# Cross-attention layers on one core: the second head group's fetch at unit 37, the context's load in parts

## Chip, cores and metric

The kernel runs on one core of one Trainium2 chip. The metric is device time in microseconds of one execution, as the median of several.

## What is computed

Two cross-attention layers over the same context, for 8 batches of 256 text rows by 256 features and a context of 1601 rows by 256 features. Cut to what matters, everything in float32:

```python
def layer0(x, ctx):                       # 16 heads of 16 features
    a = layernorm(ctx) * gamma + beta
    Q, K, V = x @ Wq.T, a @ Wk.T, a @ Wv.T
    return x + tanh(gate) * (softmax(Q K.T / 4) V) @ Wo.T

def layer1(x, ctx):
    q = layernorm(x) @ q_w + q_b
    k, v = ctx @ k_w + k_b, ctx @ v_w + v_b
    h = x + (softmax(q k.T / 4) v) @ cproj_w + cproj_b
    return h + gelu(layernorm(h) @ fc_w + fc_b) @ proj_w + proj_b
```

The mask of the first layer is all ones in the data.

## The kernel before

**Blocks and units.** One block is the attention of one layer for one batch; there are 16, numbered n = 0 to 15, even ones for layer 0, odd ones for layer 1. In the program a block is known by `n0`: 0 and 1 stand alone, 2 and 3 are the body of a loop of six passes, 14 and 15 stand alone again; -1 and 16 are a prologue and an epilogue without attention. An odd block here is n0=1 or n0=3. n0=14 is an even block by its attention, but it prepares the keys of the last odd block.

A block has 52 units: four groups of four heads (g = 0 to 3), times 13 tiles of 128 context rows. In a unit TensorE makes the scores of the tile for four heads in two halves, ScalarE takes the exponentials, and TensorE weighs the values with them one unit later. Beside that a unit holds one or two chunks: the scores of 128 queries against all 1601 keys, of which VectorE takes the maximum for the softmax. The chunks run 22 ahead, so at unit 47 those of the next block's second group begin. Two chunk buffers stand between TensorE and VectorE: a chunk waits until the maximum two chunks earlier has been taken.

**Pieces.** While block n attends, it also prepares the next one and finishes the previous one, in pieces put at fixed units by tables (`PREP0_AT`, `PREP1_AT`, `POST0_AT`, `POST1_AT`): T (transpose two tiles of the context), K(m, c) (keys of head half m, context chunk c), Q, V, WO, FC and PJ (the MLP), MX (transpose the maxima of a group; units 9, 22, 35, 48). In a block that prepares layer 1 Q is at unit 23, K(1,0) to K(1,3) at 25, 28, 30 and 33, FC at 12, 17, 27 and 32, V(0) at 36.

**A K piece's way.** TensorE multiplies; ScalarE saves a rounded first part into one of two buffers `parts`; VectorE makes the remainder and a second part, GpSimd the third (bf16 parts that add up to the float32 value); SyncE stores the three to HBM (`split_out`, 384 KB). A piece uses the buffer of the piece before the last, so ScalarE's save waits until that store has landed.

**SyncE's queue.** SyncE issues nearly all DMAs, in program order, each after its waits: `split_out`; `maxima_move` (a store, a wait for it, a load); `fetch_keys` and `fetch_queries`, which read a head group's parts back into the operands `kst` and `qst` (7 and 6 DMAs); `ctx_load`, which reads a batch's context into `ctxn`; x and the output. `FETCH_AT` gives the units at which the first, second and third group of the next block are fetched; the fourth is fetched as the next block starts. `CTX_LOAD_AT` gives the unit of the context's load in even and in odd blocks.

**Who reads the context.** The context that an odd block loads is first read in the same block by VectorE: its statistics (`ctx_stat_tiles`), two tiles at each of the units of `STATS_AT`, the first pair at unit 31, after that unit's maximum and ahead of the next ones:

```python
STATS_AT = {31: 0, 32: 1, 34: 2, 36: 3, 38: 4, 40: 5, 44: 6}
```

The context that an even block loads (the same batch's, unnormalized) is first read by TensorE, in piece T(0) at unit 1 of the next block.

Of the kernel before, what the change touches and what calls it, by code (L numbers as in the profile page):

```python
# [29 lines left out]
B, T, S, D, H, DH, FF = 8, 256, 1601, 256, 16, 16, 1024  # L30
NT = -(-S // P)
LAST = S - (NT - 1) * P
FULL = (NT - 1) * P
# [48 lines left out]
STATS_AT = {31: 0, 32: 1, 34: 2, 36: 3, 38: 4, 40: 5, 44: 6}  # L82

CTX_LOAD_AT = (43, 23)

FIRST = ([("XT",)] + [("T", k) for k in range(7)] + [("K", 0, c) for c in range(4)]
         + [("Q",), ("V", 0), ("V", 1), ("V", 2), ("V", 3), ("V", 4), ("K", 1, 0), ("K", 1, 1), ("MX", NG), ("V", 5),
# [2 lines left out]
FIRST_CHUNKS = {("MX", NG): range(16), ("V", 5): range(16, 18), ("K", 1, 2): range(18, 20),  # L90
                ("K", 1, 3): range(20, 21), ("V", 6): range(21, 16 + EARLY)}

FETCH_AT = (24, 26, 40)


class Block:
# [96 lines left out]
def chunk_cols(c):  # L193
    return 4 * P if c < 3 else LAST
# [27 lines left out]
def build(nc, x, ctx, mask, Wq0, Wk0, Wv0, Wo0, gamma0, beta0, gate, ln1_w, ln1_b, q_w, q_b, k_w, k_b, v_w, v_b,  # L222
# [11 lines left out]
    with es:  # L234
        def sb(name, shape, dt=F32):
            return es.enter_context(nc.sbuf_tensor(name, shape, dt))

        def sem(name):
            return es.enter_context(nc.semaphore(name))
# [22 lines left out]
        ctxn = sb("ctxn", [P, NT, D])  # L262
# [61 lines left out]
        scores_ready = sem("scores_ready")  # L324
# [12 lines left out]
        misc_ready = sem("misc_ready")  # L337
# [7 lines left out]
        ctx_in = sem("ctx_in")  # L345
# [30 lines left out]
        def hold(engine, signal, value):  # L376


            engine.wait_ge(signal, value)

        def attended_batch(blk):
            return {0: 0, 1: 1, 2: blk.i, 3: blk.i + 2, 14: 6, 15: 7}[blk.n0]

        def next_ctx(blk):

            if blk.n0 == 3:
                j = blk.i + 3
                return j - j // B
            return {-1: 1, 0: 0, 1: 2, 2: blk.i + 1}[blk.n0]
# [2 lines left out]

            return blk.i + (2 if blk.n0 == 1 else 3)

        def ctx_load(sp, blk_b, after_misc):

            if after_misc is not None:
                hold(sp, misc_ready, after_misc)
            sp.dma_start(ctxn[:, 0:NT - 1, :], ctx[blk_b, 0:FULL, :].rearrange("(p j) d -> p j d", j=NT - 1)
                         ).then_inc(ctx_in, 16)  # L400
            sp.dma_start(ctxn[0:LAST, NT - 1, :], ctx[blk_b, FULL:S, :]).then_inc(ctx_in, 16)

        @block.sync
        def _(sp):
            for dst, w in (*zip(raw_qkv, (Wq0, Wk0, Wv0)), (raw_wo, Wo0)):
                sp.dma_start(dst, w.rearrange("(c o) i -> o c i", o=P)).then_inc(raw_loaded, 16)
            sp.wait_ge(const_made, 1)
            ctx_load(sp, 0, None)
            with nc.allow_non_contiguous_dma(reason="feature vectors as columns, once"):
                for dst, src in ((c_g0, gamma0), (c_b0, beta0)):  # L410
                    sp.dma_start(dst, src.rearrange("(c p) -> p c", p=P)).then_inc(raw_loaded, 16)
# [36 lines left out]
            def place_bias_rows():  # L448

                sp.wait_ge(row_saved, 2)  # L450
                for l in range(2):
                    sp.dma_start(wo[l][DH:DH + 1, 0, :], bias_row[:, l, :]).then_inc(rows_placed, 16)
# [23 lines left out]
            def fetch_keys(n, blk, k, blk_b, first):  # L476

                hs = slice(HG * k, HG * k + HG)
                for buf in range(2):
                    hold(sp, parts_out[buf], 16 * blk.uses_through(3 if k < 2 else 8, buf))  # L480
                if not first:
                    hold(sp, scores_ready, 104 * (n - 1) + 26 * (k + 1))
                m = k // 2
                rows = slice(DH * hs.start - P * m, DH * hs.stop - P * m)
                for j, (_, kp) in enumerate(PARTS):
                    sp.dma_start(kst[product_rows(j), hs, :], scr_k[m, kp, rows].rearrange("(h d) s -> d h s", d=DH)  # L486
                                 ).then_inc(k_in[k], 16)
                sp.dma_start(kst[RP:RP + 1, hs, :], scr_mask[blk_b].unsqueeze(0).unsqueeze(0).broadcast_to([1, HG, S])
                             ).then_inc(k_in[k], 16)

            def fetch_queries(blk, k):

                hs = slice(HG * k, HG * k + HG)
                for buf in range(2):
                    hold(sp, parts_out[buf], 16 * blk.uses_through(4 if k < 2 else 8, buf))
                m = k // 2
                rows = slice(DH * hs.start - P * m, DH * hs.stop - P * m)
                for j, (qp, _) in enumerate(PARTS):
                    sp.dma_start(qst[product_rows(j), hs, :], scr_q[qp, m, rows].rearrange("(h d) t -> d h t", d=DH)  # L499
                                 ).then_inc(q_in[k], 16)  # L500
# [13 lines left out]
            def visit(blk):  # L514
                n = blk.n
                if blk.n0 == 0:
                    place_bias_rows()
                if 0 <= blk.n0 < 16:

                    maker = Block(blk.n0 - 1, blk.i, None, 0, None, 0)  # L520
                    fetch_keys(n, maker, 3, attended_batch(blk), blk.n0 == 0)
                    fetch_queries(maker, 3)
                if blk.n0 == 0:
                    sp.dma_start(xin[1][:, :, :], x[1].rearrange("(p t) d -> p t d", t=TT)).then_inc(x_in, 16)
                units = range(UNITS) if blk.attends else [u for u in blk.at]
                for u in units:
                    piece = blk.at.get(u)
                    kind = piece[0] if piece else None
                    if kind in ("K", "Q"):
                        split_out(blk, piece)  # L530
                    if piece == ("WO", 1) and blk.post == 0 and blk.prep == 0:
                        hold(sp, misc_saved, blk.misc(piece) + 1)
                        sp.dma_start(xin[1][:, :, :], x[blk.prep_b].rearrange("(p t) d -> p t d", t=TT)
                                     ).then_inc(x_in, 16)
                    if kind == "MX":
                        if blk.post == 1 and piece[1] == NG:

                            hold(sp, y_out, 16 * (blk.post_b + 1))
                        maxima_move(blk, piece[1])
                    if blk.n0 < 14 and (u == CTX_LOAD_AT[blk.par] if blk.attends else piece == ("K", 1, 1)):  # L540
                        ctx_load(sp, next_ctx(blk), blk.misc(("T", NT // 2)) + 1)
                    if piece == ("PJ", 1):
                        hold(sp, misc_saved, blk.misc(piece) + 1)
                        sp.dma_start(out[blk.post_b].rearrange("(p t) d -> p t d", t=TT), y[:, :, :]
                                     ).then_inc(y_out, 16)
                    if blk.prep is not None and blk.attends and u in FETCH_AT:
                        fetch_keys(n + 1, blk, FETCH_AT.index(u), blk.prep_b, False)
                        fetch_queries(blk, FETCH_AT.index(u))
                    if blk.n0 < 0 and piece == ("K", 0, 3):
                        fetch_keys(n + 1, blk, 0, blk.prep_b, True)  # L550
                    if blk.n0 < 0 and piece == ("Q",):
                        fetch_queries(blk, 0)
                        fetch_keys(n + 1, blk, 1, blk.prep_b, True)
                        fetch_queries(blk, 1)
                    if blk.n0 < 0 and piece == ("K", 1, 3):
                        fetch_keys(n + 1, blk, 2, blk.prep_b, True)
                        fetch_queries(blk, 2)

            walk(visit)
            sp.wait_ge(y_out, 16 * B)  # L560

# [257 lines left out]
        def _(dve):  # L819
# [79 lines left out]
            def ctx_stat_tiles(blk, js, ahead):  # L899

                if js[0] == 0:
                    dve.wait_ge(ctx_in, 32 * (blk.n + 1 + ahead))
                    if blk.n0 < 0:
                        dve.wait_ge(const_made, 1)
                for j in js:
                    ins = dve.bn_stats(st[:, j, :], ctxn[:, j, :])
                if js[-1] == NT - 1:
                    ins.then_inc(ctx_stats, 1)
# [81 lines left out]
            def visit(blk):  # L990
                if not blk.attends and blk.prep == 0:
                    ctx_stat_tiles(blk, range(NT), 1)
                    ctx_var_all(blk.prep_b)
                    fold_first()
                    ctx_apply(dve, blk, range(NT))
# [57 lines left out]
        def _(pe):  # L1053
# [98 lines left out]
            def do_piece(blk, piece):  # L1152
# [4 lines left out]
                if kind == "T":  # L1157
                    k = piece[1]
                    js = range(2 * k, min(2 * k + 2, NT))
                    if blk.prep == 0:  # L1160
                        pe.wait_ge(ctx_normed, NT * blk.prep_b + js[-1] + 1)
                    elif k == 0:
                        pe.wait_ge(ctx_in, 32 * (blk.n + 2))
                    for j in js:
                        r = tile_rows(j)
                        for c in range(CH):
# [3 lines left out]
                elif kind == "K":  # L1170
                    mo, ck = piece[1:]
                    w = chunk_cols(ck)
# [4 lines left out]
                elif kind == "V":  # L1177
                    k = piece[1]
# [110 lines left out]
```

## Time and profile before

| | us |
|---|---|
| median of three runs | 2037.35 |
| the three runs | 2036.52, 2037.35, 2040.63 |
| the profiled execution | 2044.37 |
| its span | 2042.5 |
| TensorE busy | 1960.1 (96%) |
| VectorE busy | 1417.5 (69%) |
| ScalarE busy | 1298.0 (64%) |
| GpSimd busy | 424.1 (21%) |

The span is what the profile shows of the execution, from its first to its last instruction. An engine is busy while it executes; register, branch, semaphore and DMA-issuing instructions are not counted. Matmuls overlap and their ends are modelled, so a busy TensorE is not TensorE at its peak. Engines are called PE (TensorE), PEld (its weight loads), DVE (VectorE), ACT (ScalarE), POOL (GpSimd) and SP or SPq (SyncE and its DMA issues) in rows.

### The profile page before, as it was taken

Reading aid. Unit: us, or ns where it says so; the run is one execution under the profiler, and the core shown is the slowest. Engines: PE = TensorE matmul, PEld = TensorE weight load, DVE = VectorE, ACT = ScalarE, POOL = GpSimd, SP = SyncE. Lnnn points to the kernel's source line nnn. Section 1 sums busy time; section 2 is a strip of 40 time slices with the busy share of each in tenths; the row PEclk is TensorE's granted clock in tenths of the full one; section 3 lists DMA queues with packets and bytes.
Section 4 is the critical chain, followed back from the end, with each engine's and each line's share of the span. In section 5 each row is a group of like instructions: output and inputs, shape, how many; then the busy total and the mean of one; then the engine's idle time right before and its main releaser. Section 6 shows DMA issues by size and latency. Waiting matters only on the chain.

```text
span 2042.5 us, 38305 instructions
## 1 busy us (share of the span) xinstructions
PE 1960.1 (96%) x14940; PEld 1053.3 (52%) x14940; DVE 1417.5 (69%) x2389; ACT 1298.0 (64%) x2327; POOL 424.1 (21%) x441
## 2 busy tenths in 40 slices
PE   5899999999999999999999999999999999999996
PEld 4345545455554545555554555545555554554544
DVE  3677777767677776777767676686767777676742
ACT  2166656667666675667756676666766667665773
POOL 2041113103141132311232022310323103111110
PEclk8799989999999999999999999999999999999998
DMA  6435152341515242251522515143241525214100
GB/s 150 126 83 150 45 140 54 97 107 58 123 43 129 68 126 60 54 150 37 138 63 71 130 35 149 41 112 92 79 102 51 129 60 139 63 37 114 30 7 6
DMA packets 142698, 176.01 MB, mean 86 GB/s; under 512 B 35092, under 2 KB 113085, under 8 KB 140469
## 3 DMA queue, kind: packets, MB, share of 16 engines
q1 hardware_dynamic: 140373, 170.67, 32.0%
q10 hardware_dynamic: 2144, 2.90, 0.6%
q8 instruction: 118, 1.93, 0.4%
q14 instruction: 63, 0.52, 0.1%
HBM read 125.33 MB, written 48.16 MB: 85 GB/s over the span
## 4 chain that ended last, share of the span: by engine, by line
PE 76%; DVE 6%; SPq 5%; ACT 5%; DMA 4%; POOL 3%; issue 2%; ACTq 0%
PE p_sc L1114 18%; PE p_acc L1147 18%; PE p_mx L1134 14%; PE p_misc L1182 9%; PE p_misc L1175 6%; DMA scr_k<-parts 3%; PE p_misc L1220 2%; PE p_misc L1208 2%; PE p_misc L1168 2%; DVE maxes L869 2%; SPq L499 2%; SPq L486 2%; PE p_misc L1214 2%; ACT prob L779 2%; DVE rest L949 2%
## 5 line engine op out<-in xcount | busy, mean ns | idle before, releaser
L869 DVE TENSOR_REDUCE maxes<-p_mx 128x1 f32<-128x802 f32 x1024 | 985.7, 984 | 336.1 <-PE p_mx L1134 332.1
L779 ACT ACTIVATE prob<-p_sc 128x512 f32<-128x512 f32 (+1 forms) x1664 | 963.1, 596 | 328.7 <-PE p_sc L1114 326.7
L1114 PE MATMUL p_sc<-qst,kst 100*128 100x256 bf16 (+1 forms) x3328 | 647.3, 276 | 23.3 <-ACT prob L779 22.1
L1134 PE MATMUL p_mx<-kst,qst 97*128 97x401 bf16 x2048 | 528.0, 339 | 10.1 <-DVE maxes L869 9.2
L1147 PE MATMUL p_acc<-prob,vals 128*17 128x256 f32 x6656 | 523.1, 386 | 0.2
L1114 PEld LDWEIGHTS p_sc<-qst,kst 100*128 100x128 bf16 (+1 forms) x3328 | 262.0, 99 | 505.5 <-ACT prob L779 215.1
L622 POOL TENSOR_TENSOR parts<-rest,parts 128x512 bf16<-128x512 f32 (+1 forms) x144 | 139.7, 970 | 638.5 <-DVE parts L960 638.4
L1147 PEld LDWEIGHTS p_acc<-prob,vals 128*17 128x17 f32 x6656 | 110.4, 95 | 243.4 <-issue 195.2
L1134 PEld LDWEIGHTS p_mx<-kst,qst 97*128 97x128 bf16 x2048 | 192.9, 99 | 54.3 <-DVE maxes L869 26.3
L1182 PE MATMUL p_misc<-wv,ctxt 128*128 128x256 f32 x800 | 193.5, 383 | 2.0 <-DVE rest L949 2.0
L1175 PE MATMUL p_misc<-ctxt,wk 128*128 128x512 f32 x488 | 191.1, 514 | 1.4 <-ACT vals L733 0.7
L643 POOL TENSOR_TENSOR o_t<-o_raw,o_den 128x256 f32<-128x256 f32 x64 | 46.6, 729 | 628.0 <-DVE o_den L897 628.0
L1182 PEld LDWEIGHTS p_misc<-wv,ctxt 128*128 128x128 f32 x800 | 144.3, 188 | 23.9 <-DVE rest L949 2.4
L949 DVE SCALAR_TENSOR_TENSOR rest<-p_misc,cols,parts 128x512 f32<-128x512 f32 x122 | 76.7, 629 | 109.7 <-ACT parts L715 108.2
L733 ACT ACTIVATE vals<-p_misc 128x512 f32<-128x512 f32 (+1 forms) x108 | 61.1, 566 | 139.9 <-PE p_misc L1182 139.9
L715 ACT ACTIVATE parts<-p_misc,cols 128x512 bf16<-128x512 f32 x122 | 72.3, 593 | 110.7 <-PE p_misc L1175 89.3
L897 DVE RECIPROCAL o_den<-o_den 128x128 f32<-128x128 f32 x128 | 120.4, 942 | 0.1
L591 POOL TENSOR_SCALAR ctxn<-ctxn,mv,rstd 128x256 f32<-128x256 f32 x91 | 110.0, 1222 | 0.8
L1175 PEld LDWEIGHTS p_misc<-ctxt,wk 128*128 128x128 f32 x488 | 81.7, 191 | 53.7 <-issue 44.8
L1208 PE MATMUL p_misc<-wo,o_t 128*128 128x256 f32 x248 | 60.5, 387 | 3.6 <-issue 3.6
L1168 PE MATMUL p_misc<-ident,ctxn 128*128 128x128 f32 (+1 forms) x398 | 60.8, 272 | 3.0 <-POOL ctxn L591 1.2
L1214 PE MATMUL p_misc<-x_t,wfc 128*128 128x256 f32 x240 | 59.2, 391 | 1.4 <-ACT x_t L738 0.7
(143 smaller groups left out, 1084.3 us busy)
## 6 DMA issues: line engine op xcount, KB each, us to landing
kst<-scr_k SPq DMA_DIRECT2D x384, 200.1 KB
scr_k<-parts SPq DMA_DIRECT2D x96, 384.0 KB, 3.1
ctxn<-in_ctx_dram SPq DMA_DIRECT2D x16, 1536.0 KB
qst<-scr_q SPq DMA_DIRECT2D x384, 32.0 KB, 2.9
scr_q<-parts SPq DMA_DIRECT2D x16, 384.0 KB, 3.1
xin<-in_x_dram SPq DMA_DIRECT2D x8, 256.0 KB, 2.8
out_dram<-y SPq DMA_DIRECT2D x8, 256.0 KB, 2.0
scr_k<-parts SPq DMA_DIRECT2D x32, 48.8 KB, 2.3
```

The costliest lines, as they stand in the source:

```text
L591: engine.tensor_scalar(ctxn[:, j, :], ctxn[:, j, :], mv[:, j, 0:1], rstd[:, j:j + 1], ALU.subtract, ALU.mult).then_inc(ctx_normed, 1)
L622: pool.tensor_tensor(parts[buf][:, 2, 0:w], rest[:, buf, 0:w], parts[buf][:, 1, 0:w], ALU.subtract).then_inc(low_ready, 1)
L779: act.activation(prob[0:rows, u % 2, 2 * half:2 * half + 2, :].rearrange("p h t -> p (h t)"), p_sc[0:rows, half, :], ACT.Exp).then_inc(exp ...
L869: dve.tensor_reduce(maxes[:, c:c + 1], p_mx[:, c % 2, :, 0:CW], AX.XY, ALU.max).then_inc(chunk_done, 1)
L897: dve.reciprocal(o_den[:, half], o_den[:, half]).then_inc(den_step, 1)
L949: dve.scalar_tensor_tensor(out=rest[:, buf, 0:w], in0=res[:, 0:w], scalar=bias, in1=parts[buf][:, 0, 0:w], op0=ALU.add, op1=ALU.subtract). ...
L1114: ins = mm(p_sc[0:rows, half, T * q:T * q + T], kst[0:RB, h, P * j:P * j + rows], qst[0:RB, h, :], start=True, stop=True)
L1134: ins = mm(p_mx[:, c % 2, w, 0:CW], qst[0:RA, h, P * t:P * t + P], kst[0:RA, h, s0:s0 + CW], start=True, stop=True)
L1147: ins = mm(p_acc[32 * q:32 * q + VW, 0:T], vals[par][0:rows, j, h, :], prob[0:rows, u % 2, q, :], start=(j == 0), stop=(j == NT - 1))
L1168: ins = nc.tensor.transpose(res[:, o:o + r], ctxn[0:r, j, P * c:P * c + P], ident[0:r, 0:r])
L1175: ins = mm(res[:, 0:w], wk[blk.prep][:, c, P * mo:P * mo + P], rhs, start=(c == 0), stop=(c == CH - 1))
L1182: ins = mm(res[0:r, o:o + D], ctxt[:, j, c, 0:r], wv[blk.prep][:, c, :], start=(c == 0), stop=(c == CH - 1))
```

## The change

The second group's fetch is made at unit 37 instead of 26 and the third's at 41 instead of 40. The context's load, before one transfer of 12 tiles and one of the last 65 rows, becomes four transfers of three tiles and that of the last rows; in a block with attention they stand two units apart, at units 23, 25, 27, 29 and 31 of an odd block and 43 to 51 of an even one, each behind a wait for the scores of the unit before. The first load (at the start) and the second (in the prologue) are made in the same five transfers, one behind the other. The readers wait for all five.

```diff
--- before.py
+++ after.py
@@ -82,6 +82,8 @@
 STATS_AT = {31: 0, 32: 1, 34: 2, 36: 3, 38: 4, 40: 5, 44: 6}
 
 CTX_LOAD_AT = (43, 23)
+CTX_PARTS = 4
+CTX_STEP = 2
 
 FIRST = ([("XT",)] + [("T", k) for k in range(7)] + [("K", 0, c) for c in range(4)]
          + [("Q",), ("V", 0), ("V", 1), ("V", 2), ("V", 3), ("V", 4), ("K", 1, 0), ("K", 1, 1), ("MX", NG), ("V", 5),
@@ -90,7 +92,7 @@
 FIRST_CHUNKS = {("MX", NG): range(16), ("V", 5): range(16, 18), ("K", 1, 2): range(18, 20),
                 ("K", 1, 3): range(20, 21), ("V", 6): range(21, 16 + EARLY)}
 
-FETCH_AT = (24, 26, 40)
+FETCH_AT = (24, 37, 41)
 
 
 class Block:
@@ -392,20 +394,23 @@
 
             return blk.i + (2 if blk.n0 == 1 else 3)
 
-        def ctx_load(sp, blk_b, after_misc):
-            if after_misc is not None:
-                hold(sp, misc_ready, after_misc)
-            sp.dma_start(ctxn[:, 0:NT - 1, :], ctx[blk_b, 0:FULL, :].rearrange("(p j) d -> p j d", j=NT - 1)
+        def ctx_load(sp, blk_b, k):
+            if k == CTX_PARTS:
+                sp.dma_start(ctxn[0:LAST, NT - 1, :], ctx[blk_b, FULL:S, :]).then_inc(ctx_in, 16)
+                return
+            w = (NT - 1) // CTX_PARTS
+            js = slice(w * k, w * k + w)
+            sp.dma_start(ctxn[:, js, :], ctx[blk_b, 0:FULL, :].rearrange("(p j) d -> p j d", j=NT - 1)[:, js, :]
                          ).then_inc(ctx_in, 16)
-            sp.dma_start(ctxn[0:LAST, NT - 1, :], ctx[blk_b, FULL:S, :]).then_inc(ctx_in, 16)
 
         @block.sync
         def _(sp):
             for dst, w in (*zip(raw_qkv, (Wq0, Wk0, Wv0)), (raw_wo, Wo0)):
                 sp.dma_start(dst, w.rearrange("(c o) i -> o c i", o=P)).then_inc(raw_loaded, 16)
             sp.wait_ge(const_made, 1)
-            ctx_load(sp, 0, None)
+            for k in range(CTX_PARTS + 1):
+                ctx_load(sp, 0, k)
             with nc.allow_non_contiguous_dma(reason="feature vectors as columns, once"):
                 for dst, src in ((c_g0, gamma0), (c_b0, beta0)):
                     sp.dma_start(dst, src.rearrange("(c p) -> p c", p=P)).then_inc(raw_loaded, 16)
@@ -537,8 +542,13 @@
 
                             hold(sp, y_out, 16 * (blk.post_b + 1))
                         maxima_move(blk, piece[1])
-                    if blk.n0 < 14 and (u == CTX_LOAD_AT[blk.par] if blk.attends else piece == ("K", 1, 1)):
-                        ctx_load(sp, next_ctx(blk), blk.misc(("T", NT // 2)) + 1)
+                    for k in range(CTX_PARTS + 1):
+                        if blk.n0 < 14 and (u == CTX_LOAD_AT[blk.par] + CTX_STEP * k if blk.attends else piece == ("K", 1, 1)):
+                            if k == 0:
+                                sp.wait_ge(misc_ready, blk.misc(("T", NT // 2)) + 1)
+                            if blk.attends:
+                                sp.wait_ge(scores_ready, 104 * n + 2 * u)
+                            ctx_load(sp, next_ctx(blk), k)
                     if piece == ("PJ", 1):
                         hold(sp, misc_saved, blk.misc(piece) + 1)
                         sp.dma_start(out[blk.post_b].rearrange("(p t) d -> p t d", t=TT), y[:, :, :]
@@ -899,7 +909,7 @@
             def ctx_stat_tiles(blk, js, ahead):
 
                 if js[0] == 0:
-                    dve.wait_ge(ctx_in, 32 * (blk.n + 1 + ahead))
+                    dve.wait_ge(ctx_in, 16 * (CTX_PARTS + 1) * (blk.n + 1 + ahead))
                     if blk.n0 < 0:
                         dve.wait_ge(const_made, 1)
                 for j in js:
@@ -1160,7 +1170,7 @@
                     if blk.prep == 0:
                         pe.wait_ge(ctx_normed, NT * blk.prep_b + js[-1] + 1)
                     elif k == 0:
-                        pe.wait_ge(ctx_in, 32 * (blk.n + 2))
+                        pe.wait_ge(ctx_in, 16 * (CTX_PARTS + 1) * (blk.n + 2))
                     for j in js:
                         r = tile_rows(j)
                         for c in range(CH):
```

In the rows below, which show the order of instructions, the names are those of the tensors: `scr_k` and `scr_q` hold the stored parts of keys and queries, `kst` and `qst` the operands, `scr_max` the maxima, `ctxn` the context. First SyncE in the first odd block (n0=1), from Q's store on (the loop's odd blocks read alike). Before:

```order
L464 DMA scr_q<-parts 128x6x256
L399 DMA ctxn<-in_ctx_dram 128x3072
L401 DMA ctxn<-in_ctx_dram 65x256
L486 DMA kst<-scr_k 16x4x1601 x6
L488 DMA kst<-scr_mask 1x4x1601
L499 DMA qst<-scr_q 16x4x256 x6
L473 DMA scr_k<-parts 128x3x512
L486 DMA kst<-scr_k 16x4x1601 x6
L488 DMA kst<-scr_mask 1x4x1601
L499 DMA qst<-scr_q 16x4x256 x6
L473 DMA scr_k<-parts 128x3x512 x2
L473 DMA scr_k<-parts 128x3x65
```

And now:

```order
L469 DMA scr_q<-parts 128x6x256
L404 DMA ctxn<-in_ctx_dram 128x768
L491 DMA kst<-scr_k 16x4x1601 x6
L493 DMA kst<-scr_mask 1x4x1601
L504 DMA qst<-scr_q 16x4x256 x6
L478 DMA scr_k<-parts 128x3x512
L404 DMA ctxn<-in_ctx_dram 128x768 x2
L478 DMA scr_k<-parts 128x3x512
L404 DMA ctxn<-in_ctx_dram 128x768
L478 DMA scr_k<-parts 128x3x512
L400 DMA ctxn<-in_ctx_dram 65x256
L478 DMA scr_k<-parts 128x3x65
```

The second group's 13 DMAs (`kst`, `scr_mask`, `qst`) have left the place between the first and second of the four stores `scr_k<-parts`, and the parts of the context (`128x768`, at the end `65x256`) stand between the stores instead; the last part comes behind the third store.

Then SyncE in the even block n0=0, from the store of K(1,3) on. Before:

```order
L473 DMA scr_k<-parts 128x3x65
L486 DMA kst<-scr_k 16x4x1601 x6
L488 DMA kst<-scr_mask 1x4x1601
L499 DMA qst<-scr_q 16x4x256 x6
L399 DMA ctxn<-in_ctx_dram 128x3072
L401 DMA ctxn<-in_ctx_dram 65x256
L508 DMA scr_max<-max_rows 24x128
L511 DMA qst<-scr_max 3x1024
```

And now:

```order
L478 DMA scr_k<-parts 128x3x65
L491 DMA kst<-scr_k 16x4x1601 x6
L493 DMA kst<-scr_mask 1x4x1601
L504 DMA qst<-scr_q 16x4x256 x6
L491 DMA kst<-scr_k 16x4x1601 x6
L493 DMA kst<-scr_mask 1x4x1601
L504 DMA qst<-scr_q 16x4x256 x6
L404 DMA ctxn<-in_ctx_dram 128x768 x3
L513 DMA scr_max<-max_rows 24x128
L516 DMA qst<-scr_max 3x1024
L404 DMA ctxn<-in_ctx_dram 128x768
L400 DMA ctxn<-in_ctx_dram 65x256
```

The second group's fetch, which stood further up, is now between that store and the third group's, and the context's fourth and fifth parts come behind the move of the maxima of unit 48.

Last VectorE, in the first odd block of the changed kernel, from K(1,2) at unit 30 on, with what each row waits for:

```order
L959 SCALAR_TENSOR_TENSOR rest<-p_misc,cols,parts 128x512 [waits low_ready,high_ready]
L970 CAST parts<-rest 128x512 [waits misc_saved]
L879 TENSOR_REDUCE maxes<-p_mx 128x1 [waits chunk_ready]
L916 BN_STATS st<-ctxn 128x6 [waits ctx_in]
L916 BN_STATS st<-ctxn 128x6
L879 TENSOR_REDUCE maxes<-p_mx 128x1 [waits chunk_ready]
L916 BN_STATS st<-ctxn 128x6 x2
L879 TENSOR_REDUCE maxes<-p_mx 128x1 [waits chunk_ready]
L886 TENSOR_REDUCE neg_max<-maxes 128x8 [waits chunk_done]
```

These rows and their order are those of before; what has moved is the last of the transfers that the first BN_STATS, at unit 31, waits for.

## Rows read from the trace of the kernel before

**Rows 1.** The page, part 1, whole span: busy time, share, instructions by engine.

```profile
PE 1960.1 (96%) x14940; PEld 1053.3 (52%) x14940; DVE 1417.5 (69%) x2389; ACT 1298.0 (64%) x2327; POOL 424.1 (21%) x441
```

**Rows 2.** Waits over the whole span: engine, line, awaited, us in total, times, longest.

```profile
ACT parts L715 <- DMA scr_k<-parts: 33.5, 14, 11.3
```

**Rows 3.** Timeline of TensorE, six stretches: start, us, instruction, idle before and releaser.

```profile
285.92 0.39 PE L1114 MATMUL p_sc<-qst,kst 100*128 100x256 bf16 x2 [2.89 <-ACT prob L779]
...
522.41 0.39 PE L1114 MATMUL p_sc<-qst,kst 100*128 100x256 bf16 x2 [0.66 <-ACT prob L779]
...
1005.69 0.39 PE L1114 MATMUL p_sc<-qst,kst 100*128 100x256 bf16 x2 [1.07 <-ACT prob L779]
1012.77 0.39 PE L1114 MATMUL p_sc<-qst,kst 100*128 100x256 bf16 x2 [0.28 <-ACT prob L779]
...
1017.10 0.63 PE L1147 MATMUL p_acc<-prob,vals 128*17 128x256 f32 x8
...
1730.69 0.39 PE L1114 MATMUL p_sc<-qst,kst 100*128 100x256 bf16 x2 [1.01 <-ACT prob L779]
...
1860.77 0.49 PE L1114 MATMUL p_sc<-qst,kst 100*128 100x256 bf16 x2 [4.16 <-ACT prob L779]
...
1868.23 0.63 PE L1147 MATMUL p_acc<-prob,vals 128*17 128x256 f32 x8
```

**Rows 4.** Timeline of ScalarE at the saves of key projections, three blocks.

```profile
284.69 0.69 ACT L715 ACTIVATE parts<-p_misc,cols 128x512 bf16<-128x512 f32 x1 [5.30 <-DMA scr_k<-parts]
...
1004.46 0.69 ACT L715 ACTIVATE parts<-p_misc,cols 128x512 bf16<-128x512 f32 x1 [1.16 <-DMA scr_k<-parts]
...
1859.91 0.32 ACT L715 ACTIVATE parts<-p_misc,cols 128x65 bf16<-128x65 f32 x1 [5.07 <-DMA scr_k<-parts]
```

**Rows 5.** Timeline of SyncE's DMA issues, an odd block and block n0=14.

```profile
988.13 0.54 SPq L399 DMA_DIRECT2D ctxn<-in_ctx_dram  x1
...
997.99 0.52 SPq L473 DMA_DIRECT2D scr_k<-parts  x1
...
1008.23 5.34 SPq L473 DMA_DIRECT2D scr_k<-parts  x3
...
1855.94 5.62 SPq L473 DMA_DIRECT2D scr_k<-parts  x3
```

**Rows 6.** Timeline of VectorE, then GpSimd, in the same odd block.

```profile
1005.97 0.43 DVE L960 CAST parts<-rest 128x512 bf16<-128x512 f32 x1
...
1007.21 0.74 DVE L906 BATCH_NORM_STATS2 st<-ctxn 128x6 f32<-128x256 f32 x2
...
1011.49 0.17 DVE L885 TENSOR_TENSOR max_parts<-neg_max,max_parts 128x8 bf16<-128x8 f32 x1
...
1012.27 0.29 DVE L949 SCALAR_TENSOR_TENSOR rest<-p_misc,cols,parts 128x65 f32<-128x65 f32 x1 [0.62 <-ACT parts L715]
...
1006.47 1.16 POOL L622 TENSOR_TENSOR parts<-rest,parts 128x512 bf16<-128x512 f32 x1 [4.58 <-DVE parts L960]
```

**Rows 7.** Timeline of TensorE, the transposition of the maxima at unit 35.

```profile
1013.10 0.23 PE L1224 MATMUL p_misc<-ident_h,max_parts 128*24 128x128 bf16 x1
```

**Rows 8.** SyncE's waits; the chain at 48.93 (start, us); SyncE's timeline after it.

```profile
SPq L511 <- DMA scr_max<-max_rows: 88.0, 64, 3.4
...
48.93 3.04 DMA scr_k<-parts
...
48.93 0.89 SPq L473 DMA_DIRECT2D scr_k<-parts  x2
52.60 0.62 SPq L486 DMA_DIRECT2D kst<-scr_k  x1
```

**Rows 9.** Windows: us, busy time by engine, TensorE's granted clock, DMA share, GB/s.

```profile
288.00:290.00 2.00, 2.00 (x12) 1.43 (x14) 2.00 (x5) 1.20 (x2) 0.00 (x0) 0.50 0.60 159
1972.00:1976.00 4.00, 3.04 (x28) 1.09 (x28) 0.21 (x1) 3.59 (x7) 1.27 (x1) 1.00 0.03 7
```

**Rows 10.** Timeline of TensorE, its first instruction.

```profile
13.77 1.94 PE L1062 MATMUL p_sc<-ident,ctxt 128*128 128x128 f32 x8 [13.77 <-DMA cols<-in_L_xattn_ln_beta_dram]
```

## The prediction

> **What bounds the kernel now.** I read the page first: TensorE is busy for 1960.1 of 2042.5 us [rows 1]. That is a queue worked off in order, with few holes, so a gain can only come from the holes, and a loss only from new ones. The list of waits then tells what this change can reach: ScalarE stands 33.5 us, in 14 waits, before it saves a key projection, for a store of an earlier projection to land (its buffer is still being read) [rows 2]. TensorE's own timeline shows which of these reach it [rows 3]. In each of the six odd blocks of the loop it has one hole of 0.66 to 1.07 us behind the stalled ScalarE, in the block shown a second one of 0.28; in the first odd block (n0=1) a hole of 2.89; in the block n0=14 one of 4.16. The rest of the 33.5 us lies in the prologue and in block 0.
>
> The cause is seen on SyncE, one queue in order [rows 5]. In an odd block it issues Q's store, the context's load (1.5 MB) at 988.13, 13 DMAs of the first head group, then the store of piece K(1,0) at 997.99, 13 DMAs of the second group, and only at 1008.23 the stores of K(1,1), K(1,2) and K(1,3). ScalarE's save of K(1,2) needs K(1,0)'s store landed: it starts at 1004.46, 6.5 us after that store was issued, having waited 1.16 [rows 4]. In n0=14 there is no context load, and the fetch alone does it: K(1,1)'s store is issued at 1855.94 [rows 5], and ScalarE's save of K(1,3) waits 5.07 for it [rows 4].
>
> After the two long holes TensorE runs at half its clock: a granted share of 0.50 in 288 to 290 us, which is the level of 1.2 GHz, against 1.00 (2.4 GHz) elsewhere in the loop, as in 1972 to 1976 [rows 9]. In n0=14 the work from 1860.77 to 1868.23 takes 7.46 us; the same work (from unit 35's scores to the weighing after V(0)) takes 4.33 in a block at full clock, 1012.77 to 1017.10 [rows 3]. So that hole costs 4.16 + 3.1 = **7.3 us**.
>
> **The fetch at unit 37 instead of 26, the third at 41.** The 26 DMAs are the same. The stores of K(1,1) to K(1,3) no longer stand behind 13 issues (1008.23 less 998.5: nearly 10 us). In n0=14 K(1,1)'s store is issued right behind K(1,0)'s, some 8 us earlier, lands after about 3 us (a store of this size took 3.04 [rows 8]) and is there before ScalarE, which stood ready at 1859.91 - 5.07 = 1854.84 [rows 4]. The hole goes whole: **-7.3 us** (-4.2 if another wait keeps the clock low). The second group's keys are first read at unit 47 of the same block, ten units later; 13 issues take about 8.5 us (9.86 for 15, 988.13 to 997.99 [rows 5]) and two units took 4.33 [rows 3], so some 20 us cover them. The third group's are read in the next block, at its unit 8. In odd blocks that fetch now also stands behind the wait for the output of the MLP at unit 41; with 19 units to go it costs nothing, and TensorE would stand for it only if SyncE were held some 20 us longer.
>
> **The context's load in parts.** K(1,0)'s store now has 0.4 MB of context ahead of it, not 1.6. By the 3.04 us it lands near 1001, before ScalarE needs it (1004.46 - 1.16 = 1003.30) [rows 4, 8]. So the 1.16 us, and the 1.07 and 0.28 us of TensorE behind it [rows 3], go away in every odd block.
>
> But the load now ends later than its reader. VectorE starts the statistics of the new context at unit 31 and waits there for all five transfers. The fifth is issued at unit 31 on SyncE, behind the store of K(1,2), and that store waits for VectorE and GpSimd to split K(1,2). Step by step in the block at 1004, with everything 1.16 us earlier:
> - VectorE's cast of K(1,2) ended at 1005.97 + 0.43, now at 1005.24; GpSimd's subtraction ended at 1006.47 + 1.16, now at 1006.47 [rows 6].
> - SyncE then issues the store and, some 0.6 us later (0.54 for an issue [rows 5]), the fifth part: 1007.1.
> - It lands after x. No row shows a 65 KB load behind a store. From below: a 6 KB store on an empty queue is waited for 88.0/64 = 1.4 us [rows 8]. From above: in the prologue two stores are issued from 48.93, the first large, the second small; the first lands after 3.04, and the next instruction that waits for both starts at 52.60, so the small one took at most 3.2 us from its own issue near 49.4 [rows 8]. That is the nearest case (a small transfer 0.5 us behind a large store); I take **x = 2.7**: landing at 1009.8.
> - VectorE has done its maximum of unit 31 by 1006.2 and stands 3.6 us. Queued behind are all maxima of later units, two of which TensorE may be ahead of, then the split of the maxima and K(1,3)'s first step, which TensorE's transposition of the maxima at unit 35 waits for.
> - From the first statistic to the last step of that split VectorE needed 1007.21 to 1011.66, then 0.29 for K(1,3) [rows 6]; without the short waits inside, with the releases, 4.65 us. TensorE's transposition so comes at 1014.45, where it came at 1013.10 [rows 7]: **+1.35 us a block**, in general x - 1.35.
>
> Bounds for the block: x = 1.4 gives 0, x = 3.2 gives 1.85; if VectorE's delay were wholly hidden, -1.35. TensorE makes the delay up nowhere, since it has no other holes. Six blocks: **+8.1 us** (0 to +11).
>
> The Trainium skill (DMA: Bandwidth & Descriptors, Queues, rings and completion order) says that a transfer's completion count lands only after every earlier write of the same DMA engine. By that the fifth part could not count before K(1,2)'s store is done, and the sum would stay at or above what x = 2.5 gives, +6.9 us for the six blocks. The bound of 3.2 us agrees with it; no row here shows a load counted behind a store.
>
> **The block n0=1.** ScalarE has less to do there and waited 5.30 [rows 4]. The store of K(1,0) now lands some 2.4 us sooner, so the statistics wait until about 288.7 and the transposition comes half a microsecond sooner than before. TensorE still has a hole, now of some 3 to 4 us in place of 2.89, so it still drops to half clock, and a V piece comes to lie in the slow stretch: about +1.3. Together **+0.8** (-3 to +3).
>
> **The rest.** At the start three more issues (0.5 each) stand ahead of the norm's vectors, for which TensorE waits until 13.77 [rows 10]. They lie in the same queue behind the weights and the whole context in either kernel, so I take the data and not the issue to set their time: +0.1, at most +1.6 were the cover gone. In even blocks the parts go out at units 43 to 51 and TensorE transposes the first tile at unit 1 of the next block, two units or some 4.3 us after the last is issued; against 2.7 us for landing that is hidden; uncovered, the price would be what landing takes beyond that, once in each pair of blocks. Two further issues a load in SyncE's idle time: nothing.
>
> **Sum**: -7.3 + 8.1 + 0.8 + 0.1 = **+1.7 us**. The profiled execution took 2044.37 us with 2042.5 of span; the three timed runs have a median of 2037.35, which is 0.34% less. I put the difference on the median: **2039 us**. Own range of this case 2033 to 2046.
>
> **Rivals.**
> A. *The forecast*: the wait moves from ScalarE to VectorE, the gain of n0=14 is given back in the six blocks. 45%.
> B. *Faster*: the fifth part lands soon, or VectorE's delay is taken up by TensorE's two units of slack. Then the six blocks give 6 x -1.35 = -8, n0=14 -7.3, n0=1 its 2.89 and the some 4 us of slow clock behind it: -22, or 2015. It decides at x of about 1.4; at x = 2 the sum is -7.3 + 3.9 + 0.8 = -2.5. For it: the 6 KB row. Against: the two stores of the prologue. 18%.
> C. *Slower, by the clock*: in the six blocks TensorE would have, by the steps above, about 1.5 us idle at unit 34, 1.4 us of work, 1.4 us idle at unit 35. If that takes it to half clock as in n0=14, each such block loses another 3.1 us: all six +18.6, the sum +20, 2058; three of them 2048. For it: the holes of 2.89 and 4.16 us did it. Against: holes of 1.07 and less did not, nor a stretch with 3.04 of 4 us busy, 1972 to 1976, at 1.00 [rows 9]. This lies between, so some blocks may drop and others not. 30%. The Trainium skill (TensorE: Matmul & The Clock Gate, HAM oscillation — how this bites in real kernels) describes a kernel whose waits take it to the lower clock anew in every tile. By that rule the time would be this case's, near 2058.
> D. *The gain of n0=14 does not come*, since another wait takes the place of K(1,3)'s: +9, 2046. 7%.
>
> **Chances.** A change under 0.2% (4 us) is what a measurement of this kernel can't tell. A lies mostly inside it (36 of 45, with 6 slower, 3 faster); B is faster (16 of 18); C slower (26 of 30); D slower (5 of 7). Faster 0.19, within 0.44, slower 0.37 (the remainders of B, C and D are put within). The range leaves out the whole of B's far end and the last of C: **2024 to 2057**.
>
> **What would show it.** Right: in the odd blocks VectorE's statistics at unit 31 wait 3 to 4 us for the context's DMA, ScalarE's waits for the stores of keys are gone, TensorE's holes lie at units 34 and 35 and are VectorE's; n0=14 has no hole and no slow stretch. Wrong: no such wait of VectorE (B); a granted clock under 1.00 in the odd blocks of the loop (C); a save still waiting for a store in n0=14 (D); or a hole at the first transposition of an odd block, which I put at nothing.

## The result: 2047.64 us, 0.4% more, and a time that follows the clock

| | before | changed |
|---|---|---|
| median, timed on the same chip | 2037.64 us (2036.41 to 2042.43, 6 runs) | 2047.64 us (2037.75 to 2052.92, 6 runs) |
| ratio | | 1.004, 95% interval 1.0025 to 1.0055 |
| the profiled execution, its span | 2044.37, 2042.5 us | 2037.75, 2035.9 us |
| mean granted clock of that execution | 0.981 | 0.984 |

The profiled execution of the changed kernel happens to be the quickest of its six, and it is quicker than the profiled one of before. So the profile shows what the change does while the clock holds, and the medians show that something else is added in most executions. Both have to be explained.

The profile after, first its list of waits over the whole span (engine, line, awaited, us in total, times, longest):

```profile
DVE st L916 <- DMA ctxn<-in_ctx_dram: 24.4, 7, 3.6
...
PE p_mx L1144 <- DVE maxes L879: 18.2, 31, 3.1
...
ACT parts L725 <- DMA scr_k<-parts: 13.8, 4, 9.3
...
PE p_misc L1234 <- DVE rest L959: 6.9, 6, 1.1
```

ScalarE's wait for stores of keys fell from 33.5 us in 14 waits [rows 2] to 13.8 in 4, of which one (3.13 us, in n0=1) is not in the prologue or block 0. A new wait stands on top: VectorE, seven times, once in each odd block that loads a context. Next SyncE's timeline in the first odd block of the loop, with the issues that were [rows 5]:

```profile
510.72 0.52 SPq L478 DMA_DIRECT2D scr_k<-parts  x1
511.29 1.11 SPq L404 DMA_DIRECT2D ctxn<-in_ctx_dram  x2
514.09 0.38 SPq L478 DMA_DIRECT2D scr_k<-parts  x1
514.51 0.49 SPq L404 DMA_DIRECT2D ctxn<-in_ctx_dram  x1
519.78 0.38 SPq L478 DMA_DIRECT2D scr_k<-parts  x1
520.20 0.46 SPq L400 DMA_DIRECT2D ctxn<-in_ctx_dram  x1
```

The stores are no longer behind 13 issues, but the fourth part of the context is issued at 514.51 and the fifth only at 520.20, right behind K(1,2)'s store. VectorE's timeline in the same place (start, us, instruction, idle before and releaser):

```profile
518.44 0.98 DVE L879 TENSOR_REDUCE maxes<-p_mx 128x1 f32<-128x802 f32 x1
522.84 0.75 DVE L916 BATCH_NORM_STATS2 st<-ctxn 128x6 f32<-128x256 f32 x2 [3.42 <-DMA ctxn<-in_ctx_dram]
...
526.97 0.28 DVE L959 SCALAR_TENSOR_TENSOR rest<-p_misc,cols,parts 128x65 f32<-128x65 f32 x1
```

It has nothing to do from 519.42 to 522.84, which is 2.64 us after the fifth part's issue. TensorE's timeline, in n0=1, in that block, and in n0=14:

```profile
287.28 0.85 PE L1144 MATMUL p_mx<-kst,qst 97*128 97x401 bf16 x2 [3.08 <-DVE maxes L879]
...
524.54 0.52 PE L1144 MATMUL p_mx<-kst,qst 97*128 97x401 bf16 x2 [1.03 <-DVE maxes L879]
...
527.30 0.23 PE L1234 MATMUL p_misc<-ident_h,max_parts 128*24 128x128 bf16 x1 [1.15 <-DVE rest L959]
...
1857.94 0.39 PE L1124 MATMUL p_sc<-qst,kst 100*128 100x256 bf16 x2
...
1862.26 0.63 PE L1157 MATMUL p_acc<-prob,vals 128*17 128x256 f32 x8
```

Each of the six odd blocks of the loop has this pair of holes, the first 0.95 to 1.18 us, the second 1.14 or 1.15, in place of the two short ones of before (0.66 to 1.07 us, then 0.28 to 0.64). In n0=14 the hole of 4.16 us is gone, and the work from unit 35's scores to the weighing after V(0) takes 4.32 us instead of 7.46. Last the granted clock in windows of 2 us (us, busy by engine, clock, DMA share, GB/s):

```profile
288.00:290.00 2.00, 2.00 (x13) 0.36 (x11) 1.82 (x7) 0.60 (x1) 0.00 (x0) 0.50 0.00 0
...
528.00:530.00 2.00, 2.00 (x19) 1.21 (x18) 2.00 (x6) 1.43 (x3) 1.10 (x1) 1.00 0.19 27
530.00:532.00 2.00, 2.00 (x17) 1.13 (x16) 1.61 (x4) 2.00 (x4) 1.28 (x1) 1.00 0.04 9
```

In this execution TensorE drops to 1.2 GHz (0.50) behind n0=1's hole, but behind none of the six pairs.

### The profile page after: what moved, and what is told of

The parts are those of the page before. It is cut to its first block, busy times and chain, and to the rows that moved or that the text cites. A ratio compares the mean times of both kernels' runs of the same rounds, so it can differ in the third digit from the quotient of the medians.

```text
span 2035.9 us, 38367 instructions
## 1 busy us (share of the span) xinstructions
PE 1954.9 (96%) x14940; PEld 1049.2 (52%) x14940; DVE 1416.0 (70%) x2389; ACT 1297.6 (64%) x2327; POOL 423.2 (21%) x441
## 4 chain that ended last, share of the span: by engine, by line
PE 80%; DVE 8%; ACT 5%; POOL 3%; DMA 2%; issue 2%; SPq 1%; ACTq 0%
PE p_acc L1157 19%; PE p_sc L1124 19%; PE p_mx L1144 15%; PE p_misc L1192 9%; PE p_misc L1185 7%; DVE maxes L879 3%; PE p_misc L1230 2%; PE p_misc L1218 2%; PE p_misc L1224 2%; PE p_misc L1178 2%; DVE rest L959 2%; ACT parts L725 2%; ACT prob L789 1%; PE p_misc L1211 1%; POOL parts L632 1%
```

## The experiments

Two theories were to be told apart. **Theory 1** is the forecast's mechanism: VectorE waits for the context's last part, TensorE for VectorE, and what the pair of holes costs depends on whether the clock then falls. **Theory 2**: the transfers themselves (more of them, or the second group's later fetch) cost the time, and the wait is hidden. Ratios are to the kernel before on the same chip, with the 95% interval; its median was 2039.59 us beside experiments 1 to 4 (16 runs) and 2040.46 beside 5 to 8 (11 runs).

**1. The changed kernel again, unedited.**

> The changed kernel unaltered, to see what its scatter (2037.75 to 2052.92 us in six executions) goes with. Theory 1 (the clock): the two holes of TensorE that VectorE's wait for the context makes in each odd block take it to half clock in some blocks and not in others, so the time follows the mean granted clock: about 2038 us at 0.984 and 2050 at 0.976 to 0.978, with half-clock stretches behind the holes in the profile where the time is high. Theory 2 (the transfers): the later fetch and the parts of the context collide differently from run to run; the time then differs at the same granted clock, and the waits for DMA differ between the two profiles by 5 us or more.

2056.13 us (2039.19 to 2059.54, 11 runs), ratio 1.0066 (1.0044 to 1.0088). The runs line up with their mean granted clock: 2039.19 us at 0.983, 2044.57 at 0.981, 2051.10 at 0.980, 2056.13 at 0.974, 2059.54 at 0.972 (in the order of the clocks some runs between 2056 and 2059 change places). The one that was profiled took 2056.13 us. TensorE's timeline in its first and last odd block of the loop, then windows behind the pairs:

```profile
528.89 0.52 PE L1144 MATMUL p_mx<-kst,qst 97*128 97x401 bf16 x2 [1.33 <-DVE maxes L879]
531.66 0.28 PE L1234 MATMUL p_misc<-ident_h,max_parts 128*24 128x128 bf16 x1 [1.15 <-DVE rest L959]
...
1754.85 0.52 PE L1144 MATMUL p_mx<-kst,qst 97*128 97x401 bf16 x2 [1.08 <-DVE maxes L879]
1757.62 0.23 PE L1234 MATMUL p_misc<-ident_h,max_parts 128*24 128x128 bf16 x1 [1.15 <-DVE rest L959]
```

```profile
532.00:534.00 2.00, 2.00 (x12) 0.46 (x11) 2.00 (x5) 0.81 (x2) 1.45 (x2) 0.50 0.18 25
534.00:536.00 2.00, 2.00 (x11) 1.29 (x8) 1.01 (x2) 1.69 (x4) 0.86 (x1) 0.50 0.04 6
...
1758.00:1760.00 2.00, 2.00 (x19) 1.10 (x18) 2.00 (x5) 1.15 (x2) 1.41 (x2) 1.00 0.21 32
```

It is the same program with nearly the same holes, but now the clock is at 0.50 behind four of the six pairs for some 6.8 us each (530 to 538 is the first), behind a fifth for half as long (1512 to 1518), and behind the last not at all. From the first pair to the last this execution needed 1754.85 - 528.89 = 1225.96 us, the earlier one 1736.75 - 524.54 = 1212.21: 13.75 more for four and a half drops, or **3.06 us a drop**. The other 4.6 us between the two executions lie mostly at the start: an early hole of 0.82 us stands at 114.26 here and at 110.57 there. The waits for DMA differ by less than the 5 us that theory 2 asked for: VectorE's for the context add up to 25.2 us here and 24.4 there, ScalarE's for stores of keys to 16.3 and 13.8.

**2. Only the fetch moved** (the context's load as before):

```diff
-FETCH_AT = (24, 26, 40)
+FETCH_AT = (24, 37, 41)
```

> Only the fetches moved, the context's load as before. Theory 1: the gain of block n0=14 comes whole (-7.3 us), the 0.7 to 1.1 us holes of the odd blocks stay, since the store of K(1,0) still stands behind the whole context; no wait of VectorE for the context. 2030 us, with little scatter. Theory 2: the fetch at unit 37 brings the scatter, so runs from 2030 to 2045.

2027.34 us (2025.39 to 2036.08, 6 runs), ratio 0.9952 (0.9935 to 0.997). This half of the change is a gain. The runs are less steady than theory 1 expected: four lie from 2025.39 to 2027.59 at a clock of 0.985 to 0.987, two at 2034.10 and 2036.08 with 0.982 and 0.979. No profile shows one of those two. In the profiled execution (2025.39) the hole of n0=14 is gone. In n0=1 ScalarE still waits 4.62 us for the store, and TensorE has two holes, six us apart, without a fall of the clock between them (timeline of TensorE, then a window):

```profile
282.81 0.39 PE L1114 MATMUL p_sc<-qst,kst 100*128 100x256 bf16 x2 [2.22 <-ACT prob L779]
...
288.79 0.23 PE L1224 MATMUL p_misc<-ident_h,max_parts 128*24 128x128 bf16 x1 [0.85 <-DVE rest L949]
```

```profile
284.00:286.00 2.00, 2.00 (x26) 1.09 (x18) 2.00 (x5) 1.72 (x4) 0.75 (x1) 1.00 0.16 54
```

The context's load in one piece still delays the stores in the loop: ScalarE waits 0.27 to 1.35 us in five of the six blocks. So the second group's later fetch by itself doesn't cost time, and the loss of the whole comes in with the load in parts.

**3. Only the load in parts** (the changed kernel with the fetch put back):

```diff
-FETCH_AT = (24, 37, 41)
+FETCH_AT = (24, 26, 40)
```

> Only the context's load in five parts, the fetches as before. Theory 1: the fifth part now stands behind the second group's fetch too, so VectorE waits longer at unit 31 (5 us or more in place of 3.5), the hole of TensorE grows past 2 us and half clock becomes the rule in the odd blocks; n0=14 keeps its hole of 4.16. 2060 us or more. Theory 2: as before the change, 2037 plus at most 5.

2102.3 us (2097.05 to 2104.93, 4 runs), ratio 1.0306 (1.029 to 1.0323). The 13 fetches now stand between the context's parts on SyncE (its timeline, then VectorE's and TensorE's):

```profile
520.03 0.49 SPq L404 DMA_DIRECT2D ctxn<-in_ctx_dram  x1
520.63 3.76 SPq L491 DMA_DIRECT2D kst<-scr_k  x6
...
533.03 0.59 SPq L400 DMA_DIRECT2D ctxn<-in_ctx_dram  x1
```

```profile
537.86 0.75 DVE L916 BATCH_NORM_STATS2 st<-ctxn 128x6 f32<-128x256 f32 x2 [9.67 <-DMA ctxn<-in_ctx_dram]
```

```profile
539.56 0.85 PE L1144 MATMUL p_mx<-kst,qst 97*128 97x401 bf16 x2 [7.29 <-DVE maxes L879]
```

VectorE's wait is nearly three times as long, TensorE's hole is 6.74 to 9.81 us in the odd blocks, and the clock falls behind every one. So a longer wait for the last part costs more, as theory 1 has it. The two halves of the change aren't independent either: the load in parts alone costs 3%, and the fetch at 37 is what keeps that to 0.4 to 0.7%.

**4. The parts one unit apart instead of two**, so that the fifth is issued at unit 27 (in even blocks at 47 instead of 51):

```diff
-CTX_STEP = 2
+CTX_STEP = 1
```

> The changed kernel with the parts one unit apart: the last at unit 27 of an odd block, ahead of the stores of K(1,1) and K(1,2). Theory 1: VectorE's wait goes, with it both holes in each of the six blocks (about 2.2 us each) and most of that of n0=1, and the clock stays at 1.00: 2015 us (2010 to 2022), scatter under 4 us. Theory 2 (the wait of VectorE costs nothing by itself, the scatter is of the transfers): 2035 to 2050 as the changed kernel.

2023.44 us (2022.51 to 2024.5, 4 runs), ratio 0.9923 (0.991 to 0.9936), at a clock of 0.985 in all four. SyncE's timeline:

```profile
507.97 0.52 SPq L478 DMA_DIRECT2D scr_k<-parts  x1
508.53 1.10 SPq L404 DMA_DIRECT2D ctxn<-in_ctx_dram  x2
509.68 0.43 SPq L400 DMA_DIRECT2D ctxn<-in_ctx_dram  x1
```

The same five transfers are issued, but the last is ahead of the stores of K(1,1) to K(1,3). VectorE doesn't wait, the pairs of holes are gone, and with them the scatter of the runs. It is 1 us above the top of what was expected: in n0=1 two parts of the context now stand ahead of K(1,0)'s store, ScalarE still waits 3.74 us there, and TensorE keeps holes of 1.33 and 0.86.

**5. Only the last part moved**, to unit 29, ahead of K(1,2)'s store (in even blocks to 49):

```diff
-u == CTX_LOAD_AT[blk.par] + CTX_STEP * k
+u == CTX_LOAD_AT[blk.par] + CTX_STEP * min(k, 3)
```

> The changed kernel with one transfer moved: the last 65 rows (65 KB) are issued with the fourth part at unit 29, ahead of K(1,2)'s store, in place of unit 31 behind it. Theory 1 (the place behind that store is the whole cost): VectorE's wait at unit 31 goes, and the time is that of the parts one unit apart, 2021 to 2026 us with little scatter. Rival (the last large part or the sum of the transfers is what is late): VectorE still waits 2 us or more, and the time stays above 2035.

2028.0 us (2024.03 to 2028.57, 6 runs), ratio 0.9937 (0.9923 to 0.9951), 2 us above what was expected. One issue of 65 KB, moved past one store, is worth 1.0 to 1.3% by the ratios (0.9937 against the changed kernel's 1.0040 and 1.0066), some 21 to 26 us. VectorE's timeline in n0=1 and in the loop's first odd block, then TensorE's and a window in n0=1:

```profile
286.76 0.75 DVE L916 BATCH_NORM_STATS2 st<-ctxn 128x6 f32<-128x256 f32 x2 [2.01 <-DMA ctxn<-in_ctx_dram]
...
522.35 0.75 DVE L916 BATCH_NORM_STATS2 st<-ctxn 128x6 f32<-128x256 f32 x2 [0.81 <-DMA ctxn<-in_ctx_dram]
```

```profile
288.46 0.52 PE L1144 MATMUL p_mx<-kst,qst 97*128 97x401 bf16 x2 [1.63 <-DVE maxes L879]
291.23 0.28 PE L1234 MATMUL p_misc<-ident_h,max_parts 128*24 128x128 bf16 x1 [1.15 <-DVE rest L959]
```

```profile
292.00:294.00 2.00, 2.00 (x13) 0.59 (x12) 1.97 (x5) 0.60 (x1) 0.00 (x0) 0.50 0.23 33
```

In five blocks of the loop a wait of 0.43 to 1.09 us remains on VectorE and reaches TensorE nowhere: here is the slack that the prediction put at two units of chunks. In n0=1 a wait of 2.01 does reach it, and the clock falls. From the hole of 0.30 us ahead of it to the next one behind it, that block takes 128.40 us (266.97 to 395.37) against 124.17 in experiment 4 (265.70 to 389.87): 4.2 of the 4.7 us between the two profiled executions. VectorE still waits although the last issue is early (SyncE's timeline in the loop's first odd block):

```profile
517.15 0.57 SPq L400 DMA_DIRECT2D ctxn<-in_ctx_dram  x1
```

The statistics start 5.20 us after this issue, where it was 2.64 behind the store in the changed kernel. So this time is no constant: here K(1,1)'s store and the fourth part, 384 KB each, are issued within the microsecond ahead.

**6. The reader moved instead of the load**: the first statistics at unit 33.

```diff
-STATS_AT = {31: 0, 32: 1, 34: 2, 36: 3, 38: 4, 40: 5, 44: 6}
+STATS_AT = {33: 0, 34: 1, 35: 2, 36: 3, 38: 4, 40: 5, 44: 6}
```

> The changed kernel with the reader moved in place of the transfer: the first three pairs of statistics at units 33, 34 and 35 in place of 31, 32 and 34. Theory 1: the last transfer lands near where unit 32's maximum ends, so VectorE waits under 1 us in place of 3.5, TensorE's holes shrink below 0.5 us and the clock stays: 2022 to 2030. Rival (the parts themselves slow the odd blocks): above 2037.

2021.58 us (2019.04 to 2023.77, 6 runs), ratio 0.9908 (0.9893 to 0.9923). Every transfer is issued as in the changed kernel; only VectorE's order differs (its timeline in the loop):

```profile
519.53 0.75 DVE L916 BATCH_NORM_STATS2 st<-ctxn 128x6 f32<-128x256 f32 x2
```

No wait is left before the statistics in the six blocks. In n0=1 one of 0.61 us is left. This settles it against theory 2: with the transfers unchanged, taking away the wait takes away the loss.

**7 and 8. The load at unit 13 of an odd block**, its five parts ahead of Q's store, once with the first group's fetch at unit 25, behind K(1,0)'s store, and once with it left at 24 (the second edit is made in 7 alone):

```diff
-CTX_LOAD_AT = (43, 23)
+CTX_LOAD_AT = (43, 13)
-FETCH_AT = (24, 37, 41)
+FETCH_AT = (25, 37, 41)
```

> A version meant to be faster: the changed kernel with the context's load of odd blocks at units 13 to 21 and the first group's fetch at 25, behind K(1,0)'s store and not ahead of it. Theory 1 (what is left after the parts one unit apart is the store of K(1,0) behind the first group's 13 DMAs: a hole of 1.33 us in the first odd block): that hole goes too, no save of a K piece waits for a store from block 1 on: 2016 to 2022 us. Rival: the store of K(1,1) takes the wait over, or the parts delay the stores of K(0,0) to K(0,3): 2024 or more.

> As the version before, but with the first group's fetch left at 24. Theory 1: the store of K(1,0) stands behind that fetch as it does with the parts one unit apart, so the hole of 1.3 us in the first odd block stays: 2020 to 2025 us. Rival: it was the context's first part that made that store late, then this is as fast as the version with the fetch at 25.

With the fetch at 25: 2021.25 us (2018.53 to 2021.77, 6 runs), ratio 0.9906 (0.9891 to 0.9921). With it at 24: 2021.16 us (2016.83 to 2022.22, 5 runs), ratio 0.9904 (0.9888 to 0.992). In neither does a save wait for a store of keys from block 1 on, and of n0=1's holes one of 0.18 or 0.23 us is left. I had put what remained of n0=1's hole down to the first group's fetch ahead of K(1,0)'s store. That fell. Here are that store and ScalarE's save of K(1,2), with the fetch still at 24 (SyncE's timeline, then ScalarE's):

```profile
273.63 4.88 SPq L504 DMA_DIRECT2D qst<-scr_q  x6
278.62 11.34 SPq L478 DMA_DIRECT2D scr_k<-parts  x4
```

```profile
281.79 0.69 ACT L725 ACTIVATE parts<-p_misc,cols 128x512 bf16<-128x512 f32 x1 [1.73 <-PE p_misc L1185]
```

Even behind the 13 fetches the store lands in time, and the save waits for TensorE's piece. So it was the context's parts ahead of the store that made it late in n0=1, not the fetches. In experiment 4 the store is issued 9.30 us after ScalarE began to save K(1,0), and the save of K(1,2) starts 3.98 later; here it is 8.11 and 3.17. So the parts hold up that store by some 1.2 us with their issues ahead of the fetches, and by at least 0.8 with a slower landing. Experiments 6, 7 and 8 can't be told apart by their times; all three are 0.9% quicker than the kernel before.

## Why the prediction held, and where its point lay wrong

**n0=14: right.** Predicted -7.3 us. Between two short holes that both timelines of TensorE have, one of 0.30 us on VectorE's maxima ahead of the key pieces and one of 0.82 later on, the kernel before took 94.92 us (1836.41 to 1931.33) and the changed one 87.54 (1837.81 to 1925.35): -7.4. Experiment 2 shows that the fetch alone does it. In experiment 1 ScalarE's save of K(1,2) waits 1.87 us for a store in this block, which the prediction gave as a sign of rival D, but the same stretch takes 87.55 there: it costs nothing.

**ScalarE's waits in the odd blocks: right.** Those in the loop are gone, the one in n0=1 fell from 5.30 us [rows 4] to 3.13. The prediction put the rest of the 33.5 us into the prologue and block 0; 1.92 of it lay in n0=1 (at 291.62) and 2.30 in n0=14 (at 1850.53), neither of them with a hole of TensorE.

**VectorE's wait: right in every link.** It was put at 3.6 us and is 3.42 to 3.62; x, the time that the fifth part takes from its issue until VectorE can start, was taken as 2.7, between bounds of 1.4 and 3.2, and is 2.64 to 2.83 in the seven blocks. The Trainium skill (DMA: Bandwidth & Descriptors, Queues, rings and completion order) has a transfer count as done only after every earlier write of the same DMA engine. The trace agrees as far as it goes: the statistics start 3.06 us after K(1,2)'s store was issued, about what such a store takes, 3.04 [rows 8]; no run put the part on an otherwise empty queue.

**The term of the six blocks, +1.35 each: over-sized.** By the same hole in the first and the sixth pass of the loop, five passes took 1604.91 - 396.98 us before, 241.6 each, and take 1605.33 - 393.26 in the profiled execution of the changed kernel, 242.4 each: +0.8 for each odd block, +5.0 for the six. The two holes were foreseen as 1.5 and 1.4 us and are about 1.1 and 1.15. More than half of the difference is in two links: from the first statistic to TensorE's transposition it takes 527.30 - 522.84 = 4.46 us, not 4.65, and VectorE's wait is 3.50 in the mean, not 3.6. The rest was not followed. Experiment 4 confirms what is gained if the holes of before go without new ones: its passes take 240.4 us each, -1.2 against the -1.35 of the bound.

**n0=1, +0.8: measured -0.5.** The stretch from 267.56 to 350.72 before (83.16 us) takes 82.67. TensorE's long hole is 3.08, beside one of 0.72 that ScalarE's remaining wait leaves, and the clock falls, as said; by windows of 2 us the half clock lasts 6.8 us (287.3 to 294.1) where before it lasted 10.2 (287.4 to 297.6), which the term had the other way.

**The start, +0.1: not to be told from scatter.** TensorE's first matmul starts at 13.06 us instead of 13.77 [rows 10], and at 12.4 in experiment 1, with the same code.

**What failed is the step that set rival C apart from the forecast.** Without falls of the clock in the loop the terms sum to -7.4 - 0.5 + 5.0 = -2.9 us, and the quickest executions, 2037.75 and 2039.19, lie where before lies. (The terms are read from an execution of before, 2044.37 us, that is slower than all six timed ones; what they are worth in a quicker one is not shown.) But of 17 executions of the changed kernel only four are within the forecast's own range of 2033 to 2046, and the median of all is 2051.10. The holes were priced as idle time, and the clock's answer to them was given 30% as a case beside it. It isn't a case beside it but a part of the term. The price was right: 3.1 us a drop was predicted, 3.06 measured. What was wrong is the weight given to [rows 9] and to the holes of 1.07 us: they were single or stood apart, and speak of one hole of about 1 us, not of two with 1.6 us of work between. And [rows 9] is one execution. The last block has the same holes of 1.15, 0.44 and 0.98 us (within 0.01) in all ten profiles; the clock stays at 1.00 behind them in four, before among these, and falls in six. In the changed kernel's first profile this stretch reads (TensorE's timeline, then a window):

```profile
1965.82 0.22 PE L1234 MATMUL p_misc<-ident_h,max_parts 128*24 128x128 bf16 x1 [0.98 <-DVE max_parts L895]
```

```profile
1968.00:1970.00 2.00, 2.00 (x14) 0.71 (x14) 0.00 (x0) 1.66 (x4) 1.26 (x1) 0.50 0.01 3
```

So a single profile could not speak against rival C. C's figures of 2048 for three drops and 2058 for six lie near the first timing's median (2047.64) and the second's top (2059.54), but no trace shows how many drops those executions had, so this may be chance. That the medians 2047.64 and 2056.13 still lie in the stated 2024 to 2057 is due to the width that rival C gave it, and not to the forecast's sum; five of the 17 executions lie above it. The Trainium skill (TensorE: Matmul & The Clock Gate, HAM oscillation — how this bites in real kernels) describes a kernel in which waits bring the lower clock back in each tile; the trace agrees in experiment 1 for four and a half of six blocks, and in the first profile for none.

**Rival B** (2015, no new wait) was wrong for this kernel, but experiments 4 to 8 show that it is close to what the change is worth when the last part comes in time: 2021 to 2028. **Rival D** was wrong: n0=14 gave its full gain.

**The first transposition of an odd block** was put at nothing, and no profile shows TensorE waiting for a transfer of the context.

**Still open** is what decides that a given pair drops the clock. The size of the holes alone doesn't: 1.11 and 1.15 us brought it in experiment 1 (at 774), 1.18 and 1.14 in the first profile (at 1737) did not, and an 0.81 followed by 1.15 brought half of one (at 1511). No experiment here took this apart.

## What to carry to other kernels

A load split into parts, all of which the reader waits for, is as late as its last part, so the last part's place in the queue is what counts: ahead of the nearest store that has to wait for other engines, or the reader behind it. A hole of 1 us in TensorE's timeline is priced by its length and by what the clock may do after it; here two close together cost some 3 us more than their sum wherever the clock fell behind them. Where timed runs of one kernel scatter by a per cent, read the granted clock of several executions before explaining any one profile.

## What the runs showed of the hardware that was not expected

The same schedule gave 2037.75 us at a granted clock of 0.984 and 2059.54 at 0.972, a difference of 1.1%. Between the two profiled executions (2037.75 and 2056.13) the count of drops behind the pairs, none against four and a half, accounts for 13.75 of the 18.4 us, and the stretch up to the hole at 110 or 114 us for 3.7.

A hole of 2.22 us, with one of 0.85 six us later, left the clock at 1.00 in experiment 2, while 1.63 and 1.15 with 1.6 us of work between took it to 0.50 in experiment 5. In these rows the longest hole was not the one that the clock answered. Each is one execution, and two of experiment 2's six runs had a lower clock, so it is not shown that the hole of 2.22 always leaves it.
